# First attention of a two-layer adaptive-norm network: the split of the row maxima moved from the vector engine to GpSimd, the copy of the values from the vector engine to ScalarE

## The reference, cut to what matters

```python
qkv = (xn @ qkv_w + qkv_b).reshape(b, s, 3, H, HD)          # H = 16, HD = 8
q, k, v = (qkv[0], qkv[1], qkv[2])
scores = jnp.einsum('bhqd,bhkd->bhqk', q, k) / np.sqrt(HD)
scores = jnp.where(causal[None, None], -jnp.inf, scores)
attn_w = jax.nn.softmax(scores, axis=-1)
attn = jnp.einsum('bhqk,bhkd->bhqd', attn_w, v)
attn = attn @ out_w + out_b
```

## Time and profile before

| | |
|---|---|
| three runs | 1115.92, 1117.45, 1124.58 us (median 1117.45) |
| the profiled execution | 1114.34 us, of which the span from first to last instruction is 1112.6 us |
| the first attention in it | about 47 to 337 us |
| one batch of it in the steady part | 15.51 us |

### The profile page before, as it was taken

How to read it: one execution, slowest core, us unless ns; L and a number is a source line. 1 busy time by engine, 2 the same in 40 slices (tenths; PEclk the granted TensorE clock), 3 DMA queues, 4 the chain that set the end, 5 groups by cost and what they waited for, 6 DMA issues and landing times.

```text
span 1112.6 us, 20326 instructions
## 1 busy us (share of the span) xinstructions
PE 977.4 (88%) x6976; PEld 582.9 (52%) x6976; DVE 631.6 (57%) x2018; ACT 546.1 (49%) x1080; POOL 451.2 (41%) x681
## 2 busy tenths in 40 slices
PE   7778999999978987899889996589996999999995
PEld 4356666666653221343534994156663644366663
DVE  2558888888823989322553442467772643344443
ACT  4505666666655544644422662347775422233331
POOL 1116766776640999000055552025551064022231
PEclk9859999999998999899989997869999899999998
DMA  6500000000001000300012243000000012011114
GB/s 212 189 0 2 3 2 2 2 2 3 3 29 58 1 1 0 151 0 0 1 37 65 75 146 94 0 1 1 2 1 2 1 41 65 0 35 42 44 30 163
DMA packets 31873, 41.91 MB, mean 38 GB/s; under 512 B 6880, under 2 KB 26720, under 8 KB 30912
## 3 DMA queue, kind: packets, MB, share of 16 engines
q1 hardware_dynamic: 27232, 31.26, 9.0%
q0 software_dynamic: 4544, 9.38, 2.6%
HBM read 29.16 MB, written 16.66 MB: 41 GB/s over the span
## 4 chain that ended last, share of the span: by engine, by line
PE 45%; DVE 4%; ACT 3%; POOL 3%; issue 3%; DMA 2%; SPq 0%; DVEq 0%; POOLq 0%
PE PS L599 5%; PE PS L577 5%; PE PS L581 5%; PE PS L300 3%; PE PS L533 3%; POOL sorted_rows L1453 3%; PE PS L535 3%; PE PS L494 3%; PE PS L542 2%; PE PS L499 2%; PE PS L590 2%; PE PS L681 2%; PE PS L668 2%; PE PS L700 2%; PE PS L711 1%
## 5 line engine op out<-in xcount | busy, mean ns | idle before, releaser
L800 ACT ACTIVATE pw<-PS 128x384 f32<-128x384 f32 x256 | 111.6, 488 | 79.0 <-PE PS L414 76.8
L1396 POOL TENSOR_SCALAR_AFFINE_SELECT pw<-pw 128x256 f32<-128x256 f32 x256 | 104.6, 433 | 95.5 <-ACT pw L800 93.7
L1031 DVE CUSTOM_DVE_ANT_0 PS<-PS,above 128x256 f32<-128x256 f32 x256 | 115.3, 450 | 47.1 <-PE PS L389 45.3
L1459 POOL DMA_INDIRECT token_rows<-xnb,slot_in x78 | 74.9, 960 | 157.7 <-ACT xnb L891 157.7
L392 PE MATMUL PS<-kf,qm 32*128 32x256 f32 x512 | 96.2, 453 | 13.3 <-DVE mx L1033 8.0
L1268 DVE TENSOR_TENSOR rsb<-sqb,PS 128x256 f32<-128x256 f32 (+1 forms) x78 | 43.2, 554 | 109.4 <-ACT sqb L884 99.5
L1446 POOL TENSOR_TENSOR XS<-XS,N 128x512 f32<-128x512 f32 x64 | 80.1, 1290 | 27.4 <-DVE N L1104 24.1
L1006 DVE TENSOR_TENSOR xnb<-PS,rsb 128x512 f32<-128x512 f32 x56 | 38.7, 691 | 87.3 <-ACT rsb L768 66.5
L1418 POOL TENSOR_SCALAR_AFFINE_SELECT pw<-pw 128x256 f32<-128x256 f32 x128 | 55.8, 471 | 71.6 <-ACT pw L921 71.6
L1033 DVE CUSTOM_DVE_ANT_0 PS<-PS,above 128x128 f32<-128x128 f32 x256 | 84.6, 330 | 0.0
L1453 POOL DMA_INDIRECT sorted_rows<-H,pos x32 | 30.9, 966 | 129.2 <-DVE pos L1249 119.8
(11 more groups left out here) (206 smaller groups left out, 2378.6 us busy)
## 6 DMA issues: line engine op xcount, KB each, us to landing
sorted_rows<-empty_rows_dram SPq DMA_DIRECT2D x2, 2535.0 KB, 14.8
slot_in<-sorted_rows SPq DMA_DIRECT2D x78, 65.0 KB, 1.9
N<-token_rows SPq DMA_DIRECT2D x16, 256.0 KB, 4.8
X<-xT_dram SPq DMA_DIRECT2D x4, 512.0 KB, 6.6
ATT<-gate_dram SPq DMA_DIRECT2D x1, 2048.0 KB, 7.5
XS<-down_dram SPq DMA_DIRECT2D x1, 2048.0 KB, 13.1
H<-up_dram SPq DMA_DIRECT2D x1, 2048.0 KB, 8.0
out_dram<-X SPq DMA_DIRECT2D x8, 256.0 KB, 3.1
```

The costliest lines, as they stand in the source:

```text
L800: nc.scalar.activation(pw[:, w % 2, j + n, :], PS[:, A_PST + (2 * v + n) % 3, 0:3 * P], ACT.Exp).then_inc(a_p, 1)
L1031: nc.vector.tensor_tensor_reduce(x[:, 0:SEQ], x[:, 0:SEQ], above[:, :], 1.0, -3e38, ALU.add, ALU.max, mx[:, 1, j, g:g + 1])
L1396: m = nc.gpsimd.affine_select(x[:, :, SEQ * k:SEQ * k + P], x[:, :, SEQ * k:SEQ * k + P], [[0, 2], [1, P]], ALU.is_ge, 0.0, base=0, channe ...
L1459: nc.gpsimd.indirect_dma_start(token_rows[l][:, :], bass.IndirectOffsetOnAxis(slot_in[:, r, D:D + 1].bitcast(mybir.dt.int32), 0), slot_out ...
```

## The change

1. `split_maxima(b)` leaves DVE (where it stood at the end of step u = 7 of batch b) and is issued by POOL at u = 0 of the next batch, behind `cut(v)` and ahead of everything of u = 1. Its four operations, their shapes and the two waits between them are the same. `mx` gets two buffers, and `maxima` at the first step of a batch waits for the split of the batch before last.
2. `values(b)` leaves DVE and is issued by ACT at u = 6 behind `exps(v)`, as a plain copy without the bias.
3. The bias of the values is folded into that of the output projection: PE transposes `vb` behind `project_qk(0)`, DVE copies one column of the result (`vcol`), PE multiplies the output weights with it at t = 4, DVE adds `col(C_OUTB)` (`outb`). `add_bias` then uses `outb`. The output weights for this product come by one more load of 64 KB, on SP between the seven loads and the sixteen.

```diff
-        mx = sb("mx", [P, 2, 4, 4])
+        mx = sb("mx", [P, 2, 2, 4, 4])
@@ SP
-                             (maskkq, a["maskkq"])):
+                             (maskkq, a["maskkq"]), (ATT[:, 0:D], a["wout"])):
@@ PE, weigh, at g == 0
                     if b:
                         pe.wait_ge(a_cp, b)
+                    else:
+                        pe.wait_ge(a_vb, 2)
@@ PE
+            def fold_bias(step):
+                if step == 0:
+                    nc.tensor.transpose(PS[:, A_PSO, 0:P], vb[:, 0, :], ident[:, :]).then_inc(a_fold, 1)
+                else:
+                    pe.wait_ge(a_vb, 1)
+                    nc.tensor.matmul(PS[:, A_PSO, SEQ:SEQ + 1], ATT[:, 0:D], vcol[:, :], start=True, stop=True).then_inc(a_fold, 1)
             project_qk(0)
+            fold_bias(0)
             for t in range(A_STEPS):
+                if t == 4:
+                    fold_bias(1)
@@ ACT
+            def values(b):
+                o = b % 2 * VAW
+                act.wait_ge(a_vps, b + 1)
+                if b >= 2:
+                    act.wait_ge(a_av, 4 * (b - 1))
+                nc.scalar.activation(region[:, o:o + 2 * HEADS0 * 32].rearrange("p (k c) -> p k c", c=32)[:, :, 16:24],
+                                     PS[:, A_PSM, 0:2 * D].rearrange("p (k d) -> p k d", d=HD0), ACT.Copy).then_inc(a_va, 1)
                 if 0 <= v < A_UNITS:
                     exps(v)
+                if u == 6 and b < BATCH:
+                    values(b)
@@ DVE
             def maxima(t):
-                g = t % 8 // 2
+                b, g = t // 8, t % 8 // 2
+                if t % 8 == 0 and b >= 2:
+                    dve.wait_ge(a_sp, b - 1)
-            def split_maxima(b):
-                ...
-            def values(b):
-                ...
+            def fold_bias(step):
+                dve.wait_ge(a_fold, step + 1)
+                if step == 0:
+                    nc.vector.tensor_copy(vcol[:, :], PS[:, A_PSO, 0:1]).then_inc(a_vb, 1)
+                else:
+                    nc.vector.tensor_tensor(outb[:, :], col(C_OUTB), PS[:, A_PSO, SEQ:SEQ + 1], ALU.add).then_inc(a_vb, 1)
-                if u == 6 and b < BATCH:
-                    values(b)
+                if t == 0 or t == 4:
+                    fold_bias(t // 4)
-                if u == 7 and b < BATCH:
-                    split_maxima(b)
@@ POOL
+            def split_maxima(b):
+                parts = mxs[:, :, :].rearrange("p n (j g s) -> p n j g s", j=4, s=HD0)
+                pool.wait_ge(a_mx, 16 * b + 16)
+                if b:
+                    pool.wait_ge(a_mt, b)
+                nc.gpsimd.tensor_copy(parts[:, :, :, :, 0], mx[:, b % 2, :, :, :]).then_inc(a_st, 1)
+                pool.wait_ge(a_st, 3 * b + 1)
+                nc.gpsimd.tensor_tensor(mxr[:, :, :, :], mx[:, b % 2, :, :, :], parts[:, :, :, :, 0], ALU.subtract).then_inc(a_st, 1)
+                nc.gpsimd.tensor_tensor(parts[:, :, :, :, 1], mx[:, b % 2, :, :, :], parts[:, :, :, :, 0],
+                                        ALU.subtract).then_inc(a_st, 1)
+                pool.wait_ge(a_st, 3 * b + 3)
+                nc.gpsimd.tensor_tensor(parts[:, :, :, :, 2], mxr[:, :, :, :], parts[:, :, :, :, 1],
+                                        ALU.subtract).then_inc(a_sp, 1)
                 if 0 <= v < A_UNITS:
                     cut(v)
+                if u == 0 and 1 <= b <= BATCH:
+                    split_maxima(b - 1)
```

More of the change, by code:

```diff
@@ L86, in adaln_kernel @@
         b1c = sb("b1c", [P, FF // P])
+        vcol = sb("vcol", [P, 1])
+        outb = sb("outb", [P, 1])
         vb = sb("vb", [P, 2, D])
@@ L168, in adaln_kernel @@
         a_qkps, a_k, a_q, a_vps, a_va = [sem("a_" + n) for n in ("qkps", "k", "q", "vps", "va")]
+        a_fold, a_vb = sem("a_fold"), sem("a_vb")
         a_s, a_mx, a_st, a_sp, a_mt, a_m = [sem("a_" + n) for n in ("s", "mx", "st", "sp", "mt", "m")]
@@ L206, in adaln_kernel @@
         LNO = 4
-        LD_A, LD_M0 = (7 + HEADS0) * 16, 11 * 16
+        LD_A, LD_M0 = (8 + HEADS0) * 16, 11 * 16
         LD_L1 = (4 + HEADS1) * 16
@@ L816, in add_bias @@
                 act.wait_ge(a_pj, b + 1)
+                if b == 0:
+                    act.wait_ge(a_vb, 2)
                 nc.scalar.activation(ATT[:, b * SEQ:(b + 1) * SEQ], PS[:, A_PSM, SEQ:2 * SEQ], ACT.Identity,
-                                     bias=col(C_OUTB)).then_inc(a_att, 1)
+                                     bias=outb[:, :]).then_inc(a_att, 1)
+            def values(b):
[5 more added lines that the diff above has]
+                                     PS[:, A_PSM, 0:2 * D].rearrange("p (k d) -> p k d", d=HD0), ACT.Copy).then_inc(a_va, 1)
             take_qk(0)
+            act.wait_ge(va_ones, 5)
             for t in range(A_STEPS):
@@ L1031, in maxima @@
                     nc.vector.tensor_tensor_reduce(x[:, 0:SEQ], x[:, 0:SEQ], above[:, :], 1.0, -3e38, ALU.add, ALU.max,
-                                                   mx[:, 1, j, g:g + 1])
+                                                   mx[:, b % 2, 1, j, g:g + 1])
                     nc.vector.tensor_tensor_reduce(x[:, SEQ:SEQ + P], x[:, SEQ:SEQ + P], above[:, P:SEQ], 1.0, -3e38,
-                                                   ALU.add, ALU.max, mx[:, 0, j, g:g + 1]).then_inc(a_mx, 1)
@@ L1050, in values @@
-            def values(b):
[L1051 to L1057, removed]
+                                                   ALU.add, ALU.max, mx[:, b % 2, 0, j, g:g + 1]).then_inc(a_mx, 1)
```

## The result

The changed kernel takes 1140.95 us (median of four runs, 1137.18 to 1143.89) beside 1118.74 for the kernel before in the same session. The ratio is 1.0213 with a 95% interval of 1.0177 to 1.0249, so it is slower, by 22.2 us between the medians and by 2.1% or about 24 us by the ratio, with an interval that lies on both sides of 2%. Forecast were 7.8 us and a range that ended at 1135.

What follows compares the result with a forecast made beforehand. PE was taken to set the pace. Thirteen late splits (+6.6), batch 1 (-0.1), batch 15 (+1.0) and the fold (+0.3) summed to +7.8 us, 1117.45 to 1125.3 us, range 1116 to 1135.

Steps and rivals of the forecast that it cites:

- two waits for `maxima`: PE's row-score loads at u = 1 (0.33 us, forecast to go) and u = 6 (0.37 us, forecast to stay).
- The fold's product: PE's added product at t = 4, ahead of the scores at 62.74, put at 0.3 us.
- Every sign that the prediction named for being wrong: Batch period under 15.5 us (cheap split or transposes not waiting) or over 16.2 (dear split or exponentials delayed).
- S: Time of the split's four 32-column operations on POOL with their two waits, taken as 1.2 us.
- The fixed part from two large sizes: POOL's 182 ns per operation, from 512 and 256 columns, giving 0.25 us for 32 columns.
- S - 0.69: Loss per batch from transposes waiting for POOL's split: 0.51 us, +6.6 over the thirteen splits of batches 2 to 14.
- A PE delay is not won back later: Within a batch, the waits at u = 6 and u = 7 start from PE's own work and shift with it.
- Batch 15: +1.0: The last split: u = 2 starts at 313.84 for 312.84, +1.0 us, with no gain from maxima.
- The granted clock is full: Reading of the first attention's steady part: full clock, PE busy 14.45 of 15.51 us a batch.
- The dearer-POOL rival: POOL's split operations cost more: loss over 1% above S = 1.43, 1134.3 us at S = 1.8; chance 0.36.
- The faster case: Both waits for maxima vanish, split hidden in POOL's free time ahead of the cut: -11.3, 1106.2 us; chance 0.04.
- the forecast's own band: S from 0.9 to 1.43 us for POOL's split, giving +3.3 to +11.2 us; chance 0.46.

Runs made afterwards that it cites:

- e2: The changed kernel with the split back on DVE at the end of u = 7: 1116.88 us beside 1115.92, ratio 1.0011.
- e3: The changed kernel with only the last of sixteen splits back on DVE: 1122.89 us beside 1115.92, ratio 1.0064.
- e5: The kernel before with four idle DVE products of 512 columns ahead of its last split: 1133.1 us beside 1117.28, ratio 1.0130.
- e6: The kernel before with four idle DVE products ahead of the split of batch 7: 1125.91 us beside 1117.28, ratio 1.0065.
- e4: The changed kernel with POOL's split issued at u = 7, behind the cut and ahead of the masked queries: 1115.34 us beside 1115.92, ratio 0.9988.
- e7: The changed kernel with the split ahead of the cut on POOL at u = 0: 1115.41 us beside 1117.28, ratio 0.9967.
- e8: The kernel before with only the split on POOL, issued at u = 7 behind the cut: 1115.99 us beside 1117.28, ratio 0.9973.
- e9: The kernel before with three idle DVE products ahead of its last split: 1119.69 us beside 1116.14, ratio 1.0022.

## Why the prediction was wrong

**What held.** PE sets the pace, and the transposing is where the split is felt. Taking `values` off DVE brought nothing (e2 is 1.0011). On ACT it took 0.39 us and delayed no exponential. One of two waits for `maxima` went away and the other stayed. The batch was forecast at 16.0 us and took 16.05: a loss of 0.51 was forecast and 0.50 came. The fold's product cost about 0.2 us where 0.3 were put (from line 342 at 61.74 to the scores at 62.74, 1.00 us, before; from line 345 at 61.98 to 63.19, 1.21, after). With the last split out of the way, by e3, the change costs 7 us; 7.8 were summed, 6.8 without that split. Every sign that the prediction named for being wrong (a period under 15.5 or over 16.2) stayed quiet, so its own test did not look where it failed.

**Two errors in the batch, which nearly cancel.** S was put at 1.2 us and is 1.34 as the sum counts it, 1.40 from first start to last end. The fixed part from two large sizes did not carry down to 32 columns for all four: the difference into fp32 took 0.27 us, near the 0.25 worked out from the earlier trace rows, but the copy took 0.32 and the two differences into strided bf16 took 0.34 each. By S - 0.69 a batch would lose 0.65 us, and u = 0 to u = 2 did grow by about that, from 204.71 - 200.92 = 3.79 us to 210.51 - 206.09 = 4.42, that is by 0.63. But 0.10 us came back in the steps behind: from u = 2 to the next u = 0 PE took 216.44 - 204.71 = 11.73 us before and 222.14 - 210.51 = 11.63 after. With marks that wander by some 0.04 us from batch to batch, the mean over the batches is a loss of 0.50. The sentence "A PE delay is not won back later" is off by that 0.1 us, and it is partly luck that 0.51 met 0.50.

In the 0.27 us of the difference into fp32, the 2.16 ns a column of the earlier trace rows give the 32 columns an estimated 0.07 and leave 0.20 as fixed part, near the 0.18 that was taken. All three differences here read with a step of 16 bytes, and this one, which writes contiguously, is near the 0.25 of the earlier trace rows without such a step. The extra 0.07 us of the other two goes with the strided bf16 write, whose type and stride are not separated here.

**The step that failed.** It is the term "Batch 15: +1.0". Its wait was sized about right: PE stood 1.44 us for the split in place of 0.32 for exponentials, and the transposes came 1.5 us later relative to the step before. The error was to take the granted clock for a constant. "The granted clock is full" was read from the earlier trace rows for the steady part and carried to a stage where it had not been looked at. The tail is work of another kind: no row scores, PE busy 15.3 of 23 us. Within 1 us of the end of that wait the granted clock went to 0.50 and stayed there for 41 us, which cost nearly 12 us in the trace. e5 puts a late last split alone into the kernel before and gets +15.8 us (interval 9 to 20), and e3 takes it alone out of the changed kernel and gets some 17 back. What the two show beyond the 12 us and the wait itself was not traced.

**What stays open.** The earlier waits were 1.3 us each (17.4 in thirteen) and left the clock up; the last was 1.44. They differ in that 0.1 us and in what PE did ahead of them, since the row scores had ended before the last one. No run separates the two. The thin work of the tail can't have brought the fall about, because it comes behind it. It can only bear on how long the lower clock lasts, and that too is argued, not shown.

What the runs show of its length is two places. In e6 the clock was at 0.50 behind the wait and at 1.00 again after some 7 us, with PE busy 96% of them; in the tail it stayed at 0.50 for 41 us, with PE busy 80% of the time. That denser work brings it back sooner is the author's reading of these two, and no run tests it.

**The rivals.** The dearer-POOL rival gave 1134 us for S = 1.8 and was the nearest in time, but for the wrong reason: S = 1.34 or 1.40 lies inside the forecast's own band. The faster case was not wrong as a mechanism in one respect: with the split done ahead of the cut a batch does shorten, by 0.28 us (e4, e7, e8), but not by 0.75. No rival had a clock that falls, though the first 37 us of the same stage run at a granted clock of 0.50 in the kernel before:

```profile
47.00:85.00 38.00, 28.39 (x137) 19.98 (x141) 17.91 (x102) 3.76 (x9) 8.04 (x10) 0.51 0.00 1
```

## What to carry to other kernels

When work moves to an engine with free time, ask what stands ahead of it in that engine's order when it becomes ready. Here, in the kernel before, the maxima were complete at 201.1 us and POOL was through its cut only at 203.7, and the same four operations one place earlier made the batch faster than before. Read the granted clock for each stage separately. Where a change adds a PE wait of the size that a lower clock followed here (1.44, 1.61 and 3.07 us), put beside its own length what the stretch behind it costs at a granted clock of 0.50: nearly 12 us here for 41 us of it. The last turn of a software pipeline deserves its own sum, because its cover is gone and its clock may go with it.

## What was unexpected of the hardware

- With one PE wait of 1.61 us at the last transposes the whole program took 15.8 us longer (e5, interval 9 to 20). Waits of 1.3 us in each of thirteen dense batches (17.4 us in total) left the clock at 1.00, one of 0.81 us at the last transposes did too (e9, up to 336 us), and one of 3.07 us amid dense work brought it down to 0.50 for about 7 us (e6).
- Behind the last transposes the lower clock (0.50) lasted 41 us in the changed kernel and in e5, with PE busy 80% of the time in the tail. In the steady part it ended within one batch, with PE busy 96%.
- The clock's rise from 0.50 to 1.00 at the start of the attention differs by some 6 us between executions of the same code (at about 85 us in e5, at about 91 in e6).
- On POOL an operation of 32 columns took 0.27 us into contiguous fp32 and 0.34 into bf16 with a stride of 8; a copy of that size took 0.32.
